# A sequence kernel in one launch: new order at its head, other loads, and a seam that keeps its tensors on the chip

## What is computed

```python
zxbcdt = jnp.einsum('bld,ed->ble', x, in_proj_w)
...
dt = jax.nn.softplus(zxbcdt[..., D_INNER + CONV_DIM:] + dt_bias)
...
h = h * dA_t[:, :, None, None] + dBx
y = jnp.einsum('bhpn,bn->bhp', h, C_t)
...
y = jnp.einsum('bld,ed->ble', y, out_proj_w) + x
...
logits = jnp.einsum('bmd,dnp->bmnp', x, phi)
dispatch = jax.nn.softmax(logits, axis=0)
bsz, m, n, p = logits.shape
combine = jax.nn.softmax(logits.reshape(bsz, m, n * p), axis=-1).reshape(bsz, m, n, p)
slots = jnp.einsum('bmd,bmnp->bnpd', x, dispatch)
y = jnp.einsum('bnpd,nde->bnpe', slots, W) + b[None, :, None, :]
out = jnp.einsum('bnpd,bmnp->bmd', y, combine)
```

## Time and profile before

| | before |
|---|---|
| median of 3 runs | 1551.91 us |
| lowest, highest | 1551.19, 1554.07 us |
| the profiled execution | 1551.86 us |
| its span, first to last instruction | 1549.8 us |
| mean granted TensorE clock | 0.959 |
| busy: TensorE, VectorE, ScalarE, GpSimd | 1432.3, 1218.3, 821.1, 792.0 us |

### The profile page before, as it was taken

One profiled execution on the slowest core, in us unless ns is written; L12 is line 12 of the kernel. 1 busy time (PEld: TensorE's weight loads), 2 busy tenths in 40 slices (PEclk: granted clock), 3 DMA queues, 4 the chain that ended last, 5 costly groups with the idle time before them and its releaser, 6 DMA issues. The chain is left out here.

```text
span 1549.8 us, 32352 instructions
## 1 busy us (share of the span) xinstructions
PE 1432.3 (92%) x10752; PEld 1259.4 (81%) x10752; DVE 1218.3 (79%) x2355; ACT 821.1 (53%) x1850; POOL 792.0 (51%) x1959
## 2 busy tenths in 40 slices
PE   6689999999999999999999999937999999879997
PEld 5458888878878878888888877827999999879997
DVE  6578889889889888888898887646888888637664
ACT  4344454454454454454454443204777767567774
POOL 1333346356355355355454452224777777567773
PEclk9589999999999999999999999957999999989999
DMA  5100000000000000000000000019666777778772
GB/s 183 61 8 8 1 15 1 14 15 1 15 15 1 15 9 7 15 5 11 15 5 12 8 4 5 8 42 249 187 182 186 195 198 195 235 274 324 301 305 72
DMA packets 140753, 131.97 MB, mean 85 GB/s; under 512 B 7377, under 2 KB 130513, under 8 KB 134097
## 3 DMA queue, kind: packets, MB, share of 16 engines
q1 hardware_dynamic: 140624, 130.37, 26.6%
HBM read 73.72 MB, written 56.62 MB: 84 GB/s over the span
## 5 line engine op out<-in xcount | busy, mean ns | idle before, releaser
L684 PE MATMUL bk<-ve_f,oe 128*128 128x128 f32 x2048 | 275.7, 279 | 0.8 <-DVE ve_f L1651 0.8
L684 PEld LDWEIGHTS bk<-ve_f,oe 128*128 128x128 f32 x2048 | 248.8, 192 | 23.1 <-issue 20.4
L2737 POOL TENSOR_TENSOR d_s<-d_ex 128x1024 f32<-128x1024 f32 x32 | 131.8, 4118 | 101.5 <-ACT d_ex L2537 101.5
L1651 DVE SCALAR_TENSOR_TENSOR ve_f<-ps_m,oT 128x512 f32<-128x512 f32 x248 | 166.3, 679 | 3.8 <-PE bk L684 2.3
L1612 DVE COPY_PREDICATED vals<-oh,bk 128x1024 f32<-128x1024 int32 x112 | 146.6, 1309 | 9.2 <-PE bk L432 7.1
L2487 PE MATMUL d_sl<-d_ex,e_prT 128*128 128x128 f32 x1024 | 136.5, 277 | 8.1 <-POOL d_ex L2754 8.1
L2421 PE MATMUL d_lg<-d_phf,d_xtf 128*128 (+1 forms) x1024 | 128.6, 287 | 14.3 <-DVE d_ex L2641 7.6
L2421 PEld LDWEIGHTS d_lg<-d_phf,d_xtf 128*128 128x128 f32 x1024 | 125.4, 203 | 15.4 <-issue 11.0
L2487 PEld LDWEIGHTS d_sl<-d_ex,e_prT 128*128 128x128 f32 x1024 | 125.8, 194 | 8.4 <-POOL d_ex L2754 8.4
L2431 PE MATMUL d_sl<-d_ex,d_xs 128*128 128x128 f32 x1024 | 121.4, 277 | 4.6 <-DVE d_ex L2652 4.6
L2431 PEld LDWEIGHTS d_sl<-d_ex,d_xs 128*128 128x128 f32 x1024 | 118.5, 194 | 5.0 <-DVE d_ex L2652 5.0
(11 more groups left out here) (363 smaller groups left out, 3730.2 us busy)
## 6 DMA issues: line engine op xcount, KB each, us to landing
logits<-d_raw SPq DMA_DIRECT2D x128, 256.0 KB, 3.4
e_lt<-logits SPq DMA_DIRECT2D x32, 1024.0 KB, 5.5
y_slots<-d_ys SPq DMA_DIRECT2D x64, 256.0 KB, 4.4
d_ex<-y_slots SPq DMA_DIRECT2D x16, 1024.0 KB, 6.9
d_w<-W SPq DMA_DIRECT2D x16, 256.0 KB, 3.5
xt_in<-xT SPq DMA_DIRECT2D x16, 128.0 KB, 2.3
x_in<-x SPq DMA_DIRECT2D x16, 128.0 KB, 2.4
ve_f<-v_exp SPq DMA_DIRECT2D x1, 2048.0 KB, 13.0
```

Of the source, the lines that this page charges most:

```text
L684: last = pe.matmul(ps_u[:, cols], oe[:, hp, e, :], mo[:, n % MO, hp, :], start=False, stop=(e == NE - 1 and hp == HP - 1), skip_group_chec ...
L1651: V.scalar_tensor_tensor(mo[:, n % MO, :, :].rearrange("p a n -> p (a n)"), chosen_of(b, c), float(NE - e), oT[:, u, c, :, :].rearrange("p ...
L2737: G.tensor_tensor(s8[:], part[:, 0:8, :], part[:, 8:16, :], ALU.add).then_inc(n, 1)
```

## The change

- **Loads of the head.** The first load of `in_w` is cut in three: 256 columns with block 0's turned input count on `first_in`, for which the first product alone waits; the other two count with the small ones. Token rows have semaphores of their own (`rows_in`), waited for by `a_res` and GpSimd's `a_xb`. Turned inputs of blocks 2 and 3 are loaded (`load_turned`) ahead of `o_exp`, and wait only for the gate product that reads the buffer.
- **Order of the head.** The hand-written lists of all engines for blocks 0 to 2 are ordered anew.
- **Memory.** Buffers of layer a lie in one tensor, `arena`, where `xtf`, `xs` and `phf` will lie when layer a is done. The eight PSUM banks are two tensors, `ps_l` and `ps_s`, which both parts share.
- **Seam.** x3 of blocks 13 to 15 (`HELD` = 13) is written straight into `xs` and `xtf`; only blocks 0 to 12 go through HBM, and their loads and phi's stand at the end of the first part's SP stream, behind waits for block 15's `a_x1h`. The first group of logits is made in the first part (`logits_ahead`): twelve products between blocks Y and Z, three and one at the end. Group 1 uses the banks of `sl`, so that it waits for nothing; group 2 waits for the copies and differences of group 0. The scalar and vector engine's first steps are written out.

```diff
+    HELD = NB - 3
+
+    AREAS = dict(cin=(NCH, L + TAPS - 1), cacc=(NCH, L), xbc=(NCH, L), am=(C, NH, P), lx=(C, NH, P), mx=(C, NH, P),
+                 xd=(C, NH, HD), xD=(C, NH, HD), tz=(C, DI), sz=(C, DI), ya=(C, DI), yg=(C, DI), yT=(2, L),
+                 xt_in=(2, L), x_in=(2, C, D))
+    arena = kept.enter_context(nc.sbuf_tensor("arena", [P, sum(math.prod(shape) for shape in AREAS.values())], F32))
+    area, at = {}, 0
+    for name, shape in AREAS.items():
+        part = arena[:, at:at + math.prod(shape)]
+        at += math.prod(shape)
+        area[name] = (part.rearrange("p (a b) -> p a b", a=shape[0]) if len(shape) == 2 else
+                      part.rearrange("p (a b c) -> p a b c", a=shape[0], b=shape[1]))
+    xtf = arena[:, 0:NB * L].rearrange("p (b c t) -> p b c t", b=NB, c=C)
+    xs = arena[:, NB * L:2 * NB * L].rearrange("p (n d) -> p n d", n=TT)
+    phf = arena[:, 2 * NB * L:2 * NB * L + S]
+    two = [kept.enter_context(nc.psum_tensor(f"ps_{n}", [P, 4, 512], F32)) for n in "ls"]
+    lg, sl = (ps[:, :, :].rearrange("p k (b s) -> p k b s", b=BB) for ps in two)
+    lg_ps = kept.enter_context(nc.semaphore("d_lg_ps"))
+    held_in = [kept.enter_context(nc.semaphore(f"held_{n}")) for n in ("phi", "turned", "rows")]
...
-        bank = [ctx.enter_context(nc.psum_tensor(f"bk{i}", [P, C, 512], F32)) for i in (0, 2)]
+        bank = [two[0][:, 2 * n:2 * n + 2, :] for n in range(2)]
         ps_v = bank
-        ps_o = ctx.enter_context(nc.psum_tensor("ps_o", [P, 512], F32))
-        ps_m = ctx.enter_context(nc.psum_tensor("ps_m", [P, 512], F32))
+        ps_o, ps_m, ps_a, ps_c = (two[1][:, n, :] for n in range(4))
         ps_u = bank[1][:, 1, 0:L]
-        ps_a = ctx.enter_context(nc.psum_tensor("ps_a", [P, 512], F32))
-        ps_c = ctx.enter_context(nc.psum_tensor("ps_c", [P, 512], F32))
 
         Y, Z = NB - 2, NB - 1
 
@@ -278,9 +296,14 @@
             return ps_m[:, 0:L] if b == 0 else ps_a[:, 0:L]
 
         def linear_of(b):
-            return bank[0][:, 0, :] if b == Z else ps_c
+            return ps_m if b == Z else ps_c
+
+        def x3_of(b, c):
+            return xs[:, C * b + c, :] if b >= HELD else x3[:, c, :]
...
-            sp.dma_start(in_w[:], in_wT).then_inc(x_in_sem[0], 16)
-            sp.dma_start(xt_in[:, 0, :], xT[:, 0:L]).then_inc(x_in_sem[0], 16)
+            sp.dma_start(in_w[:, DI:DI + 2 * P], in_wT[:, DI:DI + 2 * P]).then_inc(first_in, 16)
+            sp.dma_start(xt_in[:, 0, :], xT[:, 0:L]).then_inc(first_in, 16)
+            sp.dma_start(in_w[:, DI + 2 * P:], in_wT[:, DI + 2 * P:]).then_inc(x_in_sem[0], 16)
             for dst, src in FIRST:
                 sp.dma_start(dst[:], src).then_inc(x_in_sem[0], 16)
             for dst, src, n in FIRST_ROWS:
                 sp.dma_start(dst[:], row(src, n)).then_inc(x_in_sem[0], 16)
-            sp.dma_start(x_in[:, 0, :, :], x[0:L, :].rearrange("(c p) d -> p c d", p=P)).then_inc(x_in_sem[0], 16)
+            sp.dma_start(in_w[:, 0:DI], in_wT[:, 0:DI]).then_inc(x_in_sem[0], 16)
             for dst, src in CONSTS:
                 sp.dma_start(dst[:], src).then_inc(ready, 16)
             sp.dma_start(d_h[:], row(Dh, NH)).then_inc(ready, 16)
             sp.dma_start(xt_in[:, 1, :], xT[:, L:2 * L]).then_inc(x_in_sem[1], 16)
-            sp.dma_start(x_in[:, 1, :, :], x[L:2 * L, :].rearrange("(c p) d -> p c d", p=P)).then_inc(x_in_sem[1], 16)
+            for u in range(2):
+                sp.dma_start(x_in[:, u, :, :], x[u * L:(u + 1) * L, :].rearrange("(c p) d -> p c d", p=P)).then_inc(rows_in[u], 16)
...
+            def load_turned(b, u):
+                sp.wait_ge(q["a_z_ps"], b - 1)
+                sp.dma_start(xt_in[:, u, :], xT[:, b * L:(b + 1) * L]).then_inc(x_in_sem[u], 16)
+
             def load(b, u):
-
-                for v in (b - 1, C * (b - 1), b * L):
-                    sp.compute_val(v)
-                sp.wait_ge(rest_in, REST_IN)
-                wait(sp, q["a_xb"], b - 1)
-                wait(sp, q["a_z_ps"], b - 1)
-                wait(sp, q["a_r"], C * (b - 1))
-                sp.dma_start(xt_in[:, u, :], xT[:, bass.ds(b * L, L)]).then_inc(x_in_sem[u], 16)
-                sp.dma_start(x_in[:, u, :, :], x[bass.ds(b * L, L), :].rearrange("(c p) d -> p c d", p=P)
-                             ).then_inc(x_in_sem[u], 16)
+                if b > 3:
+                    load_turned(b, u)
+                sp.wait_ge(q["a_xb"], b - 1)
+                sp.wait_ge(q["a_r"], C * (b - 1))
+                sp.dma_start(x_in[:, u, :, :], x[b * L:(b + 1) * L, :].rearrange("(c p) d -> p c d", p=P)
+                             ).then_inc(rows_in[u], 16)
...
+            for b in (2, 3):
+                load_turned(b, b % 2)
...
-            for b in range(NB - 5, NB):
+            for b in range(NB - 5, HELD):
                 store(b)
-            sp.wait_ge(x3_stored, 32 * NB)
+            sp.wait_ge(q["a_x1h"], NB)
+            sp.wait_ge(q["a_x1l"], NB)
+            sp.dma_start(phf[:, 0:S], phi).then_inc(held_in[0], 16)
+            sp.wait_ge(x3_stored, 32 * HELD)
+            sp.dma_start(xtf[:, 0:HELD, :, :], x3T_dram.rearrange("p (b c t) -> p b c t", c=C, t=P)[:, 0:HELD, :, :]
+                         ).then_inc(held_in[1], 16)
+            sp.dma_start(xs[:, 0:C * HELD, :], x3_dram.rearrange("(n p) d -> p n d", p=P)[:, 0:C * HELD, :]
+                         ).then_inc(held_in[2], 16)
+            for n in range(3):
+                sp.wait_ge(held_in[n], 16)
...
-                        pe.wait_ge(x_in_sem[0], FIRST_IN)
+                        pe.wait_ge(first_in, 32)
...
+                if b == 0 and half == 1:
+                    pe.wait_ge(x_in_sem[0], FIRST_IN)
...
+            def logits_ahead(k, i):
+                if (k, i) == (0, 0):
+                    pe.wait_ge(held_in[0], 16)
+                    pe.wait_ge(held_in[1], 16)
+                    pe.wait_ge(q["b_pt"], HB * NB)
+                    pe.wait_ge(q["b_mo"], OUTS * NB)
+                    pe.wait_ge(q["b_oa"], NB)
+                b = BK * i + k
+                if b >= HELD:
+                    pe.wait_ge(q["c_x3t"], b + 1)
+                last = pe.matmul(lg[:, k, i, :], xtf[:, b, 0, :], phf[:, 0:P], start=(i == 0), stop=(i == BB - 1),
+                                 skip_group_check=True)
+                if i == BB - 1:
+                    last.then_inc(lg_ps, 1)
...
+            dt_rows(1)
             pe.wait_ge(ready, READY)
             a_seg(0, 0)
-            dt_rows(1)
+            dt_rows(2)
             a_seg(0, 1)
-            a_xbc(1, 1, 0, 1)
+            dt_rows(3)
             a_xt(0)
-            dt_rows(2)
+            dt_rows(4)
             a_bg(0)
...
+            for k in range(BK):
+                for i in range(BB - 1):
+                    logits_ahead(k, i)
...
+            for k in range(BK - 1):
+                logits_ahead(k, BB - 1)
             c_x3t(Z)
+            logits_ahead(BK - 1, BB - 1)
...
+                copy(xtf[:, b, :, :].rearrange("p c t -> p (c t)") if b >= HELD else x3T[:], linear_of(b)[:, 0:L]).then_inc(q["c_x3t"], 1)
...
+            dt_sums(1)
+            a_conv(1, 0, (2,))
+            a_int(0)
+            rest_prep()
+            a_y(0)
             a_conv(1, 0, (3,))
-            a_int(0)
+            dt_steps(1)
+            a_res(0, 0)
...
             rsqrt(pool, "rms", 0, 1.0 / DI, EPS, q["a_sq"], C)
+            a_am(1)
             rsqrt(pool, "ln1", 0, 1.0, EPS, norms["ln1"]["moments"], 2 * C)
...
+        def home_of(g):
+            return sl if isinstance(g, int) and g == 1 else lg
...
-            sp.dma_start(phf[:, 0:P], phi[:, 0:P]).then_inc(ready, 16)
             sp.dma_start(id_f[:], ident).then_inc(ready, 16)
-            x3T_k = x3T_dram.rearrange("p (i k c t) -> p i k c t", k=BK, c=C, t=P)
-            xtf_k = xtf[:, :, :, :].rearrange("p (i k) c t -> p i k c t", k=BK)
-            for k in range(BK):
-                sp.dma_start(xtf_k[:, :, k, 0, :], x3T_k[:, :, k, 0, :]).then_inc(x_in[k], 16)
-            sp.dma_start(xtf[:, :, 1, :], x3T_dram.rearrange("p (b c t) -> p b c t", c=C, t=P)[:, :, 1, :]
-                         ).then_inc(x_in[BK], 16)
-            sp.dma_start(phf[:, P:], phi[:, P:]).then_inc(late, 16)
             load_w(0, 0)
             load_w(1, 1)
-            sp.dma_start(xs[:], x3_dram.rearrange("(n p) d -> p n d", p=P)).then_inc(late, 16)
...
+                    if isinstance(g, int) and g == 2:
+                        pe.wait_ge(q["raw"], BK)
+                        pe.wait_ge(q["sub"], 2)
+                    elif k % 2 == 0 and not (isinstance(g, int) and g == 1):
+                        pe.wait_ge(q["raw"], BK * (g - 1) + k + 2)
+                        pe.wait_ge(q["sub"], 2 * (g - 1) + k // 2 + 1)
...
+            logits(0, 1)
+            logits(1, 0)
+            for k in range(BK):
+                slots(0, 0, 0, k)
+            logits(1, 1)
+            for k in range(BK):
```

(19 more changed lines are left out.)

366 lines of the change are left out of this document (190 added, 176 removed).

## The result

The changed kernel took 1540.12 us (median of 4 runs, 1539.74 to 1540.61), beside 1552.56 for the kernel before on the same chip (1551.19 to 1554.07). The ratio is 0.992 with a 95% interval of 0.9903 to 0.9937: 12.4 us faster, where 23.5 were forecast, and 1.1 us outside the range. The profiled execution has a span of 1538.0 us against 1549.8, so 11.8 us less.

A forecast was written before the change was run, and what follows sets the result against it. The tensor engine bounds the middle, so only time saved in the loose head and seam counts: seam 15.5 plus head 8.0 is 23.5 us off 1551.86, giving 1528.4; 8-in-10 range 1519 to 1539.

The forecast's parts named there:

- (2): Seam: twelve of sixteen products of group 0 go into the 4.8 us hole before 1011.08 and cost about nothing.
- (4): Seam: first maximum and two differences end at 1044.3; group 1, on the other PSUM tensor, runs beside them to 1046.6.
- (3): Seam: last transpose at 1037.80, a copy and one product to 1038.7, then 0.9 for the entry: 1039.6.
- The third rival: Seam entry: each engine's first instruction behind the jump waits for code, 2.1 instead of 0.9; 1.2 us less gain, 1529.6; 8%.
- The stores did not hold the third group: Seam rival: logits stores delay group 2's copies, its maximum near 1061 not 1056.6; gain 11, time 1532.9; 12%.
- (7): Seam: group 3 runs 1060.3 to 1063.9; second slot sums start at 1064.6, not 1080.13, gaining 15.5 us.
- Step (2): Head: dt products moved ahead push block 0's transposes by some 2.4 us; gated output ends near 36.3 instead of 34.92.
- Step (5): Head: residual at 42.3 plus 13.6 us of block 0's norms puts x1 at 55.9, against 65.12 before.
- step (1): Head: smaller first load brings the first product forward, but the first copy still waits for prepared weights; worth 0.
- Step (6): Head: x1 to first attention product takes 5.5 us (2.5 before), so 61.4 against 67.61: 6.2 us gained.
- Step (7): Behind the first attention product: the tensor engine idles 6.0 of 47.2 us, a third counted as saved: 1.8 us.
- The head gives nothing: Head rival: block 0's delays and one late partner on five in-order engines cancel the rest; time 1536.4; 20%.

The follow-up runs named there:

- experiment 11: Changed kernel with all 32 products of the dispatch's first group moved behind the last transpose of block 15; 1542.14 us.
- experiment 2: Changed kernel with the first group of dt products moved behind the first decay product on the tensor engine; 1535.00 us.
- experiment 3: Changed kernel with two extra unused products of 256 columns put ahead of the first group of dt products; 1536.38 us.
- experiment 7: Changed kernel with two vector engine steps swapped: the dispatch's last scaling goes ahead of the combine's first maximum; 1536.34 us.
- experiment 4: Changed kernel with the four dt product groups back at their old places, their sums, exponents and steps on other engines behind them; 1535.99 us.
- experiment 5: New seam with the old engine lists, plus smaller first load, turned inputs loaded ahead and the decay activation ahead of the first copy; 1532.08 us.
- experiment 9: Experiment 5's kernel with the scalar engine's copies of block 1's first half and btok ahead of the wait for value weights; 1531.37 us.
- experiment 10: Experiment 9's kernel with the dispatch's last scaling ahead of the combine's first maximum; 1530.25 us.
- experiment 12: Experiment 10's kernel with the load of all blocks' turned inputs issued ahead of the row loads of blocks 0 and 1; 1530.77 us.

## Why the prediction was wrong

**Seam: right, 15.9 against 15.5.** (1), (2) and the second tensor in (4) happened as written; experiment 11 shows (2) by itself. (3) was 1.1 us too late: the chain of block 15 was 0.9 shorter by the level, and the entry took 0.3 where I had chosen 0.9 (1040.11 to 1040.43 on the tensor engine). The branch whose stall the Trainium skill describes (Runtime: NRT & Kernel Launch, section Instruction fetch mechanics) cost little here: the tensor engine stood 0.32 us, and the vector engine began 1.6 us behind the last transpose, copy and product included. The scalar engine and GpSimd waited for their inputs there and show nothing. The third rival fell. (4) The scalar engine's table load of 1.28 us stood ahead of the exponentials, inside my 4.5. The stores did not hold the third group: the copies waited 0.63 us for one, and the maximum of the third group started at 1055.62 where the rival had 1061, before the 1.9 us of the head are taken off. (7) I had 1064.6; with the head's 1.9 that is 1066.5, and it was 1066.11. That it came so close is luck in part: the third maximum stood 2.9 us earlier than forecast (1055.62 less 1.9 against 1056.6), and the second scaling then took 4.42 us where I had 2.29.

**Head: the step that failed is (2), then (5).** The first copy moved after all, from 9.69 to 7.78: step (1) is worth 1.9, not 0. I had seen that the prepared weights wait for the first loads, and not that the old first product waited for the token rows besides and ended at 9.65, 0.04 us before that copy; the table load of 1.28 us right ahead of the copy is gone from there too.

Step (2) had the count right and the durations wrong. Its 2.4 us for the transposes is about what two more groups ahead of them cost at the 2.4 GHz level (1.84 us, and an estimate of 1.6 for one of 14 records), less block 1's second half that left this place (1.03). But each group took the duration of the other level: the four took 13.0 us, of which at 2.4 GHz some 6.9 would stay. The two decay products took 4.1 us instead of 2.9, y(0) 3.65 instead of 2.00, and the transposes, the B and C products and the two behind them 2.2 more together. That makes 11.1 us, and the wait of 1.42 us for the load that the dt products read stood in no step. The forecast 36.3 less 1.9 for the earlier start and with these 12.5 gives 46.9; the gated output ended at 46.92. It fits better than such a sum can be trusted, since not all of these products were waited for; but the term that was missing is the level, at which the same instructions run. Experiments 2, 3 and 7 give back only a part of it, 3.2 to 3.6 us at the output projection (46.5 to 46.9 instead of 50.09), since the level fell again in the second group; with the groups apart it starts at 42.84 (4), with the old lists at 38.5 to 43.9 (5, 9, 10, 12). What brings the level down stays open.

I took a duration from a row, and with it silently the level at which the row had been measured; the new order took the products away that had stood before and between the dt groups. Step (3) followed: residual 52.70, forecast 42.2. Step (4) was right, the wait for the load is gone. Step (5) had 13.6 us from residual to x1; with the old lists it is 16.0 (experiments 5 and 10), in the changed kernel 15.8, so its term was 2.2 us short, and the rest of the miss at x1 (68.54 against 55.9) is the late residual. In the changed kernel the two roots on POOL took 6.6 and 5.4 us where they had taken 4.4 and 4.2, and 1.2 of this came back between them. The vector and POOL order did not show in the changed kernel, since dt was early there; experiment 4 shows it as the next bound once dt is apart. Step (6): attention 71.89 instead of 61.4; its own term, 5.5 behind x1, was 2.1 too long. Step (7) was about right: of 4.3 us late at the attention, 1.9 were left at the seam, 2.4 where I had 1.8. "The head gives nothing" had the right mechanism (delays add up on five engines) and a size that was too kind.

**What no step had:** 2.3 us between dispatch and combine. The kernels with the new seam and without the swap have 35.3 to 36.4 us there, in ten profiles. Rows of the changed kernel, vector engine:

```profile
1328.98 2.29 DVE L2763 TENSOR_REDUCE e_nmx<-e_lt 128x1 f32<-128x2048 f32 x1 [4.02 <-DMA e_lt<-logits]
...
1332.16 2.29 DVE L2749 TENSOR_TENSOR d_ex<-d_ex,d_sr 128x2048 f32<-128x2048 f32 x1
```

and of the kernel before:

```profile
1341.26 2.29 DVE L2666 TENSOR_REDUCE e_nmx<-e_lt 128x1 f32<-128x2048 f32 x1 [2.65 <-DMA e_lt<-logits]
```

The maximum waited 4.02 us for its load; before the change it waited 2.65. The load landed 1.4 us later behind the expert product, and everything in order behind it: the last slot sums start 11.0 us behind that product instead of 9.7. This is 1.3 of the 2.3; 0.6 more is the duration of these slot sums (6.05 us, 5.46 before), and 0.4 stands between the turned weights and the first sums. The swap takes the scaling out of the load's way, and the slot sums start at 9.7 again (7, 10, 12). Why the load is slower with the new seam, with the same transfers around it, was not found.

## What to carry to other kernels

A duration on the tensor engine belongs to a level. Before a step is costed at "so many of such a row", look at what stood before that row on the engine and whether the new order keeps it; price it at both levels and put the difference into the range. And when a change brings loads and a new order together, cost them apart: here the loads, with one activation moved, gave 4.6 us, and the order took 8.0.

## What the runs showed of the hardware

The granted clock of a window can read 1.00 where the engine runs at 1.2 GHz: in the changed kernel it is 1.00 from 17 to 34 us, while four transposes take 1.09 us that take 0.66 at the other level; in experiment 7, whose first group took 1.95 us, the same window reads 0.61. So the reading given with the profile before, that 1.00 is the 2.4 GHz level, does not hold in the first 55 us of these traces: there the length of a known record tells the level, not the column. The mean clock of a whole run still sorts the runs of one kernel, the other way round: with this head it was 0.972 or more where the engine stayed low, since the column reads 1.00 there. Two programs with one head list, and a load 0.6 us late in one, lay 5.4 us apart at x1. And 1.8 us of useless products made a kernel 3.7 us faster by its median, one run of six excepted. On GpSimd a step on 128x2 elements that takes 0.2 us took 2.07 beside two larger operations of the vector engine.
